# Layer 1's first batch of unit 0 ahead of layer 0 of unit 1, on one core of a Trainium2 chip

## What is computed

```python
hidden = x
for i in range(3):
    z = jnp.einsum('bmd,bnd->bmnd', x, hidden).reshape(B, -1, D)
    cur = jnp.einsum('bcd,co->bod', z, Ws[i]) + bs[i][None, :, None]
    cur = jax.nn.relu(cur)
    hidden, direct = (cur[:, :100, :], cur[:, 100:, :])   # all 200 are direct in the last layer
    finals.append(direct)
return jnp.sum(jnp.concatenate(finals, axis=1), axis=-1)
```

## Time and profile before

| | before |
|---|---|
| time, median of 3 runs | 2685.38 us (2685.25 to 2686.32) |
| time of the profiled execution | 2686.64 us |
| its span | 2684.8 us |
| PE busy | 2652.3 us (99%), 17992 matmuls |
| DVE busy | 2633.4 us (98%) |
| ACT busy | 1782.6 us (66%) |
| POOL busy | 121.4 us (5%) |
| mean granted clock of PE | 0.997 of full |

### The profile page before, as it was taken

One profiled execution on the slowest core, in us unless ns is written; L12 is line 12 of the kernel. 1 busy time (PEld: TensorE's weight loads), 2 busy tenths in 40 slices (PEclk: granted clock), 3 DMA queues, 4 the chain that ended last, 5 costly groups with the idle time before them and its releaser, 6 DMA issues.

```text
span 2684.8 us, 53056 instructions
## 1 busy us (share of the span) xinstructions
PE 2652.3 (99%) x17992; PEld 2639.2 (98%) x17992; DVE 2633.4 (98%) x2593; ACT 1782.6 (66%) x2978; POOL 121.4 (5%) x148
## 2 busy tenths in 40 slices
PE   6999999999999999999999999999999999999999
PEld 4999999999999999999999999999999999999998
DVE  6999999999999999999999999999999999999998
ACT  4666666666666666666666666666666666666665
POOL 0000000000000000000000000000000000000000
PEclk8999999999999999999999999999999999999999
DMA  8555545545565555455456544554555455455542
GB/s 187 138 143 142 132 121 138 141 121 125 143 156 128 129 142 130 120 137 140 125 138 152 140 120 127 143 131 120 135 144 127 124 141 137 120 128 143 129 120 72
DMA packets 249154, 357.76 MB, mean 133 GB/s; under 512 B 30631, under 2 KB 184019, under 8 KB 248959
## 3 DMA queue, kind: packets, MB, share of 16 engines
q1 hardware_dynamic: 229091, 330.02, 47.1%
q0 software_dynamic: 18960, 25.76, 5.5%
q10 hardware_dynamic: 1008, 0.75, 0.1%
HBM read 325.98 MB, written 5.91 MB: 124 GB/s over the span
## 4 chain that ended last, share of the span: by engine, by line
PE 97%; DVE 1%; issue 1%; SPq 1%; DMA 1%; ACT 0%; DVEq 0%
PE acc L917 64%; PE acc L918 30%; PE acc L910 2%; PE turned L930 1%; DVE z_low L547 0%; DMA xb<-x_by_unit 0%; DVE z L541 0%; DMA x_by_unit<-mixed 0%; DMA x_right<-x_by_unit 0%; PE x_turned L939 0%; SPq L338 0%; ACT w_split L774 0%; SPq L340 0%; SPq L312 0%; DVE z L514 0%
## 5 line engine op out<-in xcount | busy, mean ns | idle before, releaser
L917 PE MATMUL acc<-w_split,z_high 128*128 128x400 f32 (+1 forms) x8704 | 2602.7, 367 | 20.4 <-DVE z_low L547 16.4
L918 PE MATMUL acc<-w_split,z_low 128*128 128x200 f32 (+1 forms) x8704 | 2221.8, 255 | 0.0
L726 ACT ACTIVATE z_high<-z 128x1024 fp32r<-128x1024 f32 (+2 forms) x1152 | 1165.7, 1012 | 798.1 <-PE acc L918 497.9
L918 PEld LDWEIGHTS acc<-w_split,z_low 128*128 128x128 f32 (+1 forms) x8704 | 1664.7, 191 | 0.0
L917 PEld LDWEIGHTS acc<-w_split,z_high 128*128 128x128 f32 (+1 forms) x8704 | 1637.3, 188 | 23.6 <-issue 16.1
L547 DVE TENSOR_TENSOR z_low<-z,z_high 128x1024 fp32r<-128x1024 f32 (+2 forms) x1152 | 1336.6, 1160 | 19.1 <-ACT z_high L726 6.9
L541 DVE TENSOR_TENSOR z<-mixed,xb 128x1024 f32<-128x1024 f32 (+1 forms) x1024 | 1213.2, 1185 | 1.1 <-DMA xb<-x_by_unit 0.9
L446 POOL DMA_DIRECT2D direct<-fresh_direct x129 | 113.5, 879 | 2327.6 <-ACT fresh_direct L765 2306.8
L751 ACT ACTIVATE mixed<-turned 32x128 f32<-32x128 f32 x768 | 205.4, 267 | 8.9
L748 ACT ACTIVATE mixed<-turned 96x512 f32<-96x512 f32 x256 | 150.9, 590 | 6.0 <-PE turned L930 1.9
L514 DVE TENSOR_TENSOR z<-x_left,x_right 118x896 f32<-118x896 f32 x128 | 138.6, 1083 | 3.3 <-DMA x_right<-x_by_unit 3.3
(11 more groups left out here) (30 smaller groups left out, 96.7 us busy)
## 6 DMA issues: line engine op xcount, KB each, us to landing
xb<-x_by_unit SPq DMA_DIRECT2D x378, 384.0 KB, 5.2
x_right<-x_by_unit SPq DMA_DIRECT2D x384, 136.5 KB
xb<-x_by_unit SPq DMA_DIRECT2D x384, 128.0 KB, 5.9
xb<-x_by_unit SPq DMA_DIRECT2D x126, 336.0 KB
direct<-fresh_direct POOLq DMA_DIRECT2D x115, 200.0 KB, 7.1
xb<-x_by_unit SPq DMA_DIRECT2D x128, 84.0 KB
x_left<-x_by_unit SPq DMA_DIRECT2D x384, 19.5 KB
mixed<-in_L_rec_W_dram SPq DMA_DIRECT2D x5, 600.0 KB, 6.7
```

Source lines behind the costliest of these rows:

```text
L726: nc.scalar.activation(z_high[slot % RING][0:rows, 0:n * T], z[0:rows, z_place(number, slot), 0:n * T], ACT.Copy).then_inc(high, 1)
L917: nc.tensor.matmul(a[:, 0:2 * O], z_high[slot % RING][0:rows, tok], w, start=(c == 0), stop=False, skip_group_check=True)
L918: last = nc.tensor.matmul(a[:, 0:O], z_low[slot % LOW_RING][0:rows, tok], w[:, 0:O], start=False, stop=(c == chunks - 1), skip_group_check ...
```

## The change

In the numbering of batches, 1 becomes the first batch of layer 1 of unit 0 and 2 becomes layer 0 of unit 1; 0 and 3 onwards stay.

- PE multiplies layer 1's first batch (behind the wait for the first piece of W1) ahead of layer 0 of unit 1, and the transpose of unit 1 moves from behind layer 1's second batch to behind its third.
- DVE writes the factors of layer 1's first batch ahead of `low_piece(2, 1, 1)`, and its low parts ahead of the factors of layer 0 of unit 1.
- ACT writes the hidden state of unit 0 ahead of the rounding of the second piece; `second_half` for unit 1 waits for batch 2 instead of batch 1.
- SP's wait ahead of `load_pairs(2)` is for the third product instead of the second, as the factors of layer 0 of unit 1 (which read `x_left` and `x_right`) are now the third.

No instruction of work is added or taken away.

```diff
@@ SP @@
-            sp.wait_ge(product, 2)
+            sp.wait_ge(product, 3)
             load_pairs(2)
@@ DVE @@
             fresh(0, 1).then_inc(direct_begun, 1)
-            low_piece(2, 1, 1)
 
 
             at = first(0)
             dve.wait_ge(w_low_done, 1)
-            product0(1, 1, 1)
-            product12(1, 0, 0, 0, at, at)
-            lows(1, 1, L0_ROWS, L0_CHUNKS)
+            product12(1, 0, 0, 0, 1, 1)
+            low_piece(2, 1, 1)
+            lows(1, 1, P, group_chunks(0))
+            product0(1, 2, 2)
             product12(1, 0, 0, 1, at + 1, at + 1)
-            lows(at, at, P, group_chunks(0))
+            lows(2, 2, L0_ROWS, L0_CHUNKS)
             product12(1, 0, 0, 2, at + 2, at + 2)
             lows(at + 1, at + 1, P, group_chunks(1))
             sums(0, 1, 2, 1)
@@ ACT @@
             dup(0, 1, 1)
+            hidden(0, 0, 0, 1)
             high_piece(1, 1)
-            hidden(0, 0, 0, 1)
-            highs(1, 1, L0_ROWS, L0_CHUNKS)
+            highs(1, 1, P, group_chunks(0))
 
             at = first(0)
-            highs(at, at, P, group_chunks(0))
+            highs(2, 2, L0_ROWS, L0_CHUNKS)
             highs(at + 1, at + 1, P, group_chunks(1))
-            second_half(0, 1, 1)
+            second_half(0, 1, 2)
             dup(0, 1, 2)
             high_piece(1, 2)
             highs(at + 2, at + 2, P, group_chunks(2))
@@ PE @@
             transpose(0, 1, 1)
+            pe.wait_ge(w_low_done, 2)
+            multiply(1, 1, 1, 0)
             pe.wait_ge(s_in, 1)
-            multiply(0, 1, 1)
+            multiply(0, 2, 2)
             at = first(0)
-            for g in range(GROUPS):
+            for g in range(1, GROUPS):
                 pe.wait_ge(w_low_done, 2 + g)
                 multiply(1, at + g, at + g, g)
-                if g == 1:
+                if g == 2:
                     transpose(0, 1, 2)
             multiply(0, at + GROUPS, at + GROUPS)
```

## The result

The changed kernel takes 2696.97 us (median of 6 runs, 2694.49 to 2699.69), the kernel before 2685.32 us (6 runs, 2684.91 to 2687.61). The ratio is 1.0038, with a 95% interval of 1.0028 to 1.0048: 11.65 us slower. The forecast was 2694.9 us, 9.5 us slower.

What follows compares the result with a forecast made beforehand. PE's matmuls bound the loop, so prologue delay is lost one for one. 3.7 (batch 2 late) + 4.25 (transpose) + 1.6 (clock) = 9.5 us on the median 2685.4 gave 2694.9 us; range 2691.9 to 2697.1 us.

Steps and rivals of the forecast that it cites:

- POOL's clearing: POOL clears the fourth piece's stage rows beside the low parts PE waits for: cost nil, at most 1.27 us.
- The bound: PE's matmul time bounds the loop; what the prologue loses by PE's last wait (85.6 us) is lost at the end.
- Step 1: Factors ahead of the second piece: product waits for rows of x until 38.1 us, PE starts at 42.4, 1.3 us later.
- loses its free place: DVE's rounding of the second piece, formerly done while DVE was idle, now follows the product at 39.2 for 1.83 us.
- Step 2: Batch 0 ahead of layer 0 of unit 1: the 6.77 us chain starts after 15 chunks; batch 2 is 3.7 us late.
- Steps 3 and 4: Transpose behind batch 2 delays the fourth piece's rounding 4.25 us; batch 2 at 1.2 GHz adds 1.6 us (0 to 2.1).
- The sum with 2.6 us of room: DVE's sum needing PE's result after batch 3 and layer 0 of unit 2: slow matmuls there cost none of the end.
- Step 5: SP's later release (43.2 us) delays transfers 2.5 us at no cost; POOL's clearing beside the low parts costs nil.
- The clock didn't stay up in batch 2: Rival that the clock stays up in batch 2 despite the 4.5 us gap: 7.5 to 8.3 us slower; chance 0.22.
- The early factors: Rival that rows of x land by 35.8 us and PE starts at 40.3: about 7.4 us slower; chance 0.04.
- The loop gave nothing back: Rival that shorter chunks in the loop return time, some 2690 us: chance 0.09 within 0.2%, 0.03 faster.
- Something more is late: Rival: clearing beside the low parts, or another clock fall between 76 and 85 us; 10.8 to 11.7 us slower; chance 0.05.

Runs made afterwards that it cites:

- e3: The changed kernel with DVE's rounding of the second piece put back ahead of the factors of layer 1's first batch; ratio 1.0048 to the kernel before.
- e2: The kernel before with only the transpose of unit 1 moved behind layer 1's third batch; ratio 1.0020 to the kernel before.
- e7: The changed kernel with unit 0's last rows of x loaded ahead of unit 1's pairs and the transpose back behind layer 1's second batch; 2689.24 us.
- e9: The changed kernel with 16 useless matmuls (8, 4 and 4) in PE's long gaps to keep the clock up; 2695.28 us.
- e5: The kernel before with 9 useless matmuls, 7 behind its first transpose and 2 ahead of unit 1's layer 1; 2686.52 against 2686.70 us.
- e6: The changed kernel with SP loading unit 0's last rows of x ahead of unit 1's pairs; ratio 1.0036 to the kernel before.
- e10: The kernel before with W1's second piece loaded behind pairs and rows and rounded later, plus two useless matmuls ahead of unit 1's layer 1; ratio 0.9999.

## Why the prediction was right, point by point

The forecast was 9.5 us, and 8.9 to 10.4 with its own spread; the measured 11.65 us lies above that. It is in the range (up to 2697.1 us, measured 2696.97) only because the range allowed 1.27 us for POOL's clearing, which cost nothing. The steps held in kind; the slow clock was undersized twice, and that it still fits the range is luck.

**The bound** held: the loop returned and added nothing, and what the prologue was late at its last wait was late at the end.

**Step 1** had the right start for the wrong reason in part. The product waited for the rows of x (38.56 us; 38.1 predicted), PE began at 42.80 (42.4). But the rounding that "loses its free place" was worth little: e3 puts it back and gains nothing. What makes the start late is the product at 38 us and the high and low parts behind it.

**Step 2** had the right chain: from the second half to batch 2 it was 6.74 us (50.43 to 57.17; 6.77 predicted), and 4.43 us of idle time (4.5). Mis-sized was the clock in it: I took the middle, about 4.1 us at 1.2 GHz, and it was 6.3. The 15 chunks took 7.4 us and not 6.35. With the 0.4 us of step 1 batch 2 was 5.2 us late, not 3.7. The range of 3.3 to 4.1 for batch 2's delay was too narrow; it came from two stretches, and the third was longer than both.

**Steps 3 and 4**: from batch 2 to the fourth piece 8.05 us, against 1.62 before: 6.4 us, of which 4.25 + 1.6 = 5.85 were predicted. e2 measures the transpose alone at 4.2. The clock took the whole batch, the 2.1 us of the upper bound, as the idle gap of 4.43 us was followed by 1.2 GHz like those of the earlier trace rows. Nor is that sure in every execution: in e7, behind 4.32 us of idle time, the first two chunks of batch 2 ran at 2.4 GHz and the slow stretch began then. e9 confirms the clock's total up to here, about 5 us with step 2's (3.0 in the 15 chunks, 2.2 in batch 2, less 0.5 because the chunks start later in e9). The sum at the fourth piece is 11.6 us, against 9.5: 0.4 of landing, 1.1 of the clock in step 2, 0.5 of the clock in step 4, the rest rounding.

**Behind the fourth piece** the prediction had two items wrong that cancel. The sum with 2.6 us of room had to wait after all (0.79 us, 74.69 us), because batch 3 and layer 0 of unit 2 were slow for 6 us. And something was given back, 0.75 us, because unit 1's first batch was now fast; e5 shows that in the kernel before. 11.6 + 0.86 - 0.75 = 11.7.

**Step 5** held. SP went on at 43.68 us (43.2), no reader waited for the transfers behind it. POOL cleared its rows beside the low parts:

```profile
41.58 1.26 POOL L444 MEMSET mixed<- 32x1400 f32 x1 [40.02 <-DVE w_split L495]
```

DVE's low parts at 41.44 us lasted 1.22 us, as elsewhere. The rule of the Trainium skill that was weighed (GPSIMD Engine Reference, Specifications: contention with instructions of two SBUF inputs) would have lengthened them or the clearing, and this trace doesn't show it for a clearing, which reads nothing: in the kernel before, where DVE was idle beside most of it (36.83 us), it took 1.26 us too.

**The rivals.** The clock didn't stay up in batch 2 (e9 shows what a clock up in all three stretches gives: +6.9 at the mark, +8.4 at the late transpose, about the rival's 7.5 to 8.3, which had it up in batch 2 alone). The early factors (e6, e7) don't turn the sign, as was said. The loop gave nothing back in the changed kernel. The measured 11.65 us has the price of the rival *Something more is late* (10.8 to 11.7), though by neither of its two causes: it was the same clock in the same places, for longer.

## What to carry to other kernels

Where engines run lists written by hand, ask of a batch that is moved ahead not what it waits for but what waits behind the one that it passes: here layer 0 of unit 1 fed a chain of 6.8 us through three engines, and two batches of matmuls had been its cover, where one is left. An idle gap that the new order opens is to be priced twice, once as itself and once by the clock of the work behind it, and the upper end of that price belongs in the sum when the work behind it feeds a chain. Costs of single edits don't add: each of the two was hidden in part until the other had made it bind. And a mark at the end of the prologue isn't the end of the kernel: e9 lost 1.4 of its 4.8 us behind it, so check a gain at a second place, late in the loop.

## What the runs showed of the hardware

The time at 1.2 GHz after an idle gap varied more than the trace of before had shown: 4.9 and about 3.3 us there, 6.3 us in the changed kernel from the start of dense matmuls at 42.80 us, and about 3.3 us in e7 at the same place in the order (gaps of 8.73 and 6.45 us). The length of the gap didn't settle what followed. In e5 a gap of 2.88 us was followed by 1.2 GHz at once (batch 2's first matmul took 0.67 us and not 0.42); in e7 one of 4.32 us and in e10 one of 2.51 us were followed by 0.6 us at 2.4 GHz and then 3.6 and 3.3 us at 1.2 GHz. And the clock fell for 3 us at the end of the changed kernel's profiled execution, behind waits of 0.83 and 1.53 us, and cost 1.4 us; the same waits stand in the other profiles, and the clock fell behind them in seven of the twelve.
